# Graph layers and experts on one core: segment columns computed in the instruction's own address, nine of the last ten tiles scattered in three bf16 parts, the residual added on TensorE, the last moments read from PSUM

## The reference, cut to what matters

```python
def _layernorm(x, axis=-1, eps=1e-05):
    m = jnp.mean(x, axis=axis, keepdims=True)
    v = jnp.var(x, axis=axis, keepdims=True)
    return (x - m) / jnp.sqrt(v + eps)

def _L1_gnn_ref(x_nodes, x_edges, path_coeffs, src, dst, path_indices):   # 64 paths, 16 segments of 32
    x1 = x_nodes[src].reshape(-1, N_SEG, EXTENT)
    x2 = x_edges.reshape(-1, N_SEG, EXTENT)
    i1, i2, i3 = (path_indices[:, 0], path_indices[:, 1], path_indices[:, 2])
    contrib = path_coeffs[None, :, None] * x1[:, i1, :] * x2[:, i2, :]
    edge_out = jnp.zeros((x2.shape[0], N_SEG, EXTENT), x_nodes.dtype).at[:, i3, :].add(contrib)
    out = jnp.zeros((n_nodes, OP_SIZE), x_nodes.dtype).at[dst].add(edge_out.reshape(-1, OP_SIZE))
    return out

x = x + _L0_gnn_ref(_layernorm(x), edge_index, ...)
x = x + _L0_ffn_ref(_layernorm(x)[None], ...)[0]
x = x + _L1_gnn_ref(_layernorm(x), edge_attr_512, L1_gnn_path_coeffs, src, dst, L1_gnn_path_indices)
x = x + _L1_ffn_ref(_layernorm(x)[None], L1_ffn_controller, L1_ffn_f1, L1_ffn_f2)[0]
```

## Time and profile before

| | |
|---|---|
| median of the runs | 307.92 us (307.78 to 309.34) |
| the profiled execution | 308.1 us, its span 306.2 us |
| busy in the span | PE 93%, DVE 74%, ACT 45%, POOL 16% |
| chain that ended last, by engine | PE 82%, DVE 5%, issue 5%, ACT 5% |
| first layers, up to the first path | 0 to 101 us |
| block 0, block 1, block 2 | about 101 to 148.7, 148.7 to 206.6, 206.6 to 250.7 us |
| last block's sums to the first transposes | 250.7 to 268.9 us |
| rest of the fourth layer and the store | to 306.2 us |

### The profile page before, as it was taken

One profiled execution on the slowest core, in us unless ns is written; L12 is line 12 of the kernel. 1 busy time (PEld: TensorE's weight loads), 2 busy tenths in 40 slices (PEclk: granted clock), 3 DMA queues, 4 the chain that ended last, 5 costly groups with the idle time before them and its releaser, 6 DMA issues.

```text
span 306.2 us, 5935 instructions
## 1 busy us (share of the span) xinstructions
PE 284.9 (93%) x1720; PEld 198.3 (65%) x1720; DVE 225.3 (74%) x640; ACT 137.9 (45%) x274; POOL 48.4 (16%) x49
## 2 busy tenths in 40 slices
PE   5898899999999859999999999989999999999995
PEld 4665498886444559778778676765666554578731
DVE  5968648061348759999999999999999978555231
ACT  3200241112125028875448786769988837012220
POOL 3000030000007730000489900000000022000000
PEclk9999999999999977999999999999999999999999
DMA  6799940000014752233252010003444448000001
GB/s 213 247 407 425 442 171 0 0 3 0 18 50 139 204 140 69 71 110 100 68 158 85 5 32 3 1 0 139 148 147 139 138 113 301 0 2 2 2 0 68
DMA packets 12288, 33.39 MB, mean 109 GB/s; under 512 B 3297, under 2 KB 3298, under 8 KB 12002
## 3 DMA queue, kind: packets, MB, share of 16 engines
q1 hardware_dynamic: 10338, 26.73, 24.3%
q0 software_dynamic: 1920, 6.29, 7.2%
HBM read 31.97 MB, written 1.05 MB: 108 GB/s over the span
## 4 chain that ended last, share of the span: by engine, by line
PE 82%; DVE 5%; issue 5%; ACT 5%; DVEq 1%; DMA 1%; ACTq 0%; SPq 0%
PE psum L1165 16%; PE psum L1116 14%; PE psum L1064 9%; PE psum L1168 7%; PE psum L967 5%; PE psum L1088 4%; PE psum L1093 4%; PE psum L999 3%; PE psum L1222 2%; PE psum L1247 2%; PE psum L1241 2%; PE psum L1014 2%; PE psum L1123 2%; PE psum L1156 1%; ACT prod L519 1%
## 5 line engine op out<-in xcount | busy, mean ns | idle before, releaser
L1116 PE MATMUL psum<-big,dst_oh 128*128 128x512 f32 x116 | 53.9, 593 | 0.0
L418 POOL DMA_INDIRECT big<-xn_rows,big x24 | 38.5, 1606 | 93.5 <-DMA xn_rows<-xn 48.8
L519 ACT ACTIVATE prod<-edges,coef_b 128x320 f32 (+1 forms) x65 | 35.6, 588 | 21.4 <-PE psum L1168 18.9
L864 DVE TENSOR_TENSOR prod<-big,prod 128x320 f32<-128x320 f32 (+1 forms) x65 | 34.0, 523 | 0.1
L1165 PE MATMUL psum<-prod,ident 128*128 128x128 f32 x160 | 32.2, 299 | 0.6 <-issue 0.2
L1165 PEld LDWEIGHTS psum<-prod,ident 128*128 128x128 f32 x160 | 24.9, 197 | 9.3 <-issue 7.4
L1116 PEld LDWEIGHTS psum<-big,dst_oh 128*128 128x128 f32 x116 | 20.2, 191 | 15.9 <-issue 15.8
L1064 PE MATMUL psum<-edges,big 128*128 128x256 f32 x128 | 28.3, 380 | 0.0
L874 DVE TENSOR_TENSOR big<-big,prod 128x64 f32 (+2 forms) x80 | 26.1, 326 | 1.6 <-issue 0.4
L1064 PEld LDWEIGHTS psum<-edges,big 128*128 128x128 f32 x128 | 24.1, 190 | 3.5 <-DVE edges L791 0.3
L519 ACT ACTIVATE xparts<-edges,coef_b 128x320 f32 (+1 forms) x41 | 22.5, 587 | 3.4 <-PE psum L1168 1.4
(11 more groups left out here) (195 smaller groups left out, 488.9 us busy)
## 6 DMA issues: line engine op xcount, KB each, us to landing
big<-in_w SPq DMA_DIRECT2D x3, 2048.0 KB, 15.9
edges<-in_f SPq DMA_DIRECT2D x11, 512.0 KB, 3.3
edges<-in_edge SPq DMA_DIRECT2D x1, 3584.0 KB, 23.9
edges<-in_edge SPq DMA_DIRECT2D x1, 2560.0 KB, 23.0
edges<-in_edge SPq DMA_DIRECT2D x5, 512.0 KB, 3.9
edges<-in_f SPq DMA_DIRECT2D x1, 2560.0 KB, 9.9
big<-in_gnn_w SPq DMA_DIRECT2D x1, 1024.0 KB, 6.4
xs<-in_x SPq DMA_DIRECT2D x1, 512.0 KB, 3.8
```

The source lines that it names most:

```text
L418: nc.gpsimd.indirect_dma_start(out=x1g[b % 2][:, i, :], out_offset=None, in_=xn_rows, in_offset=bass.IndirectOffsetOnAxis(ap=idx_i[:, 0, F ...
L519: nc.scalar.activation(slot(n)[:, 0:BLOCKS[b], :], edges[:, FIRST[b]:FIRST[b] + BLOCKS[b], bass.ds(single_column(words, p), U)], ACT.Copy, ...
L864: nc.vector.tensor_tensor(v, xg[:, 0:tiles, bass.ds(cols[0], U)], v, ALU.mult).then_inc(mults, 1)
L1116: last = mm(bank[2 + h], dst_oh[:, n % DR, h * P:(h + 1) * P], tile_sums(b, t), start=n == 0, stop=False)
```

## The change

It has three parts.

Columns at the instruction. `column` no longer multiplies by 32. The segment number goes straight into the access pattern (`segment`), and the builder puts the factor into the address. `product_columns` is gone: `multiply` works out its column itself, right in front of its instruction, and so after DVE's wait for ACT's slot has been set in program order. PE's column ranges are written in the same way.

The last block. `SPLIT` is 9 instead of 5: only the first tile is scattered in fp32. ACT begins with the parts as soon as the sums are done, copies PE's sums after the second tile, and waits for that copy in front of tile 5, the first one whose sums came from PE (`KEPT_AT`). `sum_parts` takes the whole of `x1g[1]`.

The residual. Two fp32 matmuls with the identity put `xs` into banks 2 and 3 ahead of the first scattered tile, during block 1. At the end DVE takes the moments of each half, and normalises it, straight from PSUM; ACT copies the halves back into `xs` (`keep_x3`), one between the two roots and one behind its transposed copy. PE waits for both copies ahead of line 1199's matmuls.

```diff
-    SPLIT = 5
+    SPLIT = 9
+    KEPT_AT = BLOCKS[2] - KEPT[2] - (BLOCKS[2] - SPLIT)
...
-            return psum[:, bass.ds(k * PT + 4 * 512, PT * U)]
+            return psum[:, 4 * 512:].rearrange("p (s e) -> p s e", e=PT * U)[:, bass.ds(k, 1), :].rearrange("p o e -> p (o e)")
...
-            return nc.s_assert_within(v * U, 0, (NS - 1) * U,
+            return nc.s_assert_within(v, 0, NS - 1,
                                       skip_runtime_bounds_check_because="segment numbers are below the segments")
+
+        def segment(ap, seg):
+            return ap.rearrange("p t (s u) -> p t s u", u=U)[:, :, bass.ds(seg, 1), :].rearrange("p t o u -> p t (o u)")
...
-            copy_sums(NB - 1, 0, 8)
             act.wait_ge(sums, NP * NB)
-            act.wait_ge(block_out, banks_before(NB))
+            act.wait_ge(scattered, FIRST[2])
             for i in range(SPLIT + 1):
+                if i == 2:
+                    copy_sums(NB - 1, 0, 8)
+                if i == KEPT_AT:
+                    act.wait_ge(block_out, banks_before(NB))
...
-            for h in range(H):
-                root_of_variance(3, h)
+            def keep_x3(h):
+                act.wait_ge(xn_ready, 3 * H + h + 1)
+                nc.scalar.activation(xs[:, h, :], bank[2 + h], ACT.Copy).then_inc(x3_ready, 1)
+            root_of_variance(3, 0)
+            keep_x3(0)
+            root_of_variance(3, 1)
             copy_xnT(2, xnT2)
+            keep_x3(1)
...
-            def product_columns(n):
-                b, p = divmod(n, NP)
...
-                cols = [first_column(words[b], p)]
...
-                return [moved(dve, c, (NS - 1) * U) for c in cols]
...
-                nc.vector.tensor_tensor(v, xg[:, 0:tiles, bass.ds(cols[0], U)], v, ALU.mult).then_inc(mults, 1)
+                nc.vector.tensor_tensor(v, segment(xg[:, 0:tiles, :], first_column(words[b], p)), v, ALU.mult).then_inc(mults, 1)
...
-            multiply(0, product_columns(0))
-            cols = product_columns(1)
+            multiply(0)
             for n in range(NP * NB):
                 if n + 1 < NP * NB:
-                    multiply(n + 1, cols)
-                if n + 2 < NP * NB:
-                    cols = product_columns(n + 2)
+                    multiply(n + 1)
                 add(n)
...
             for h in range(H):
                 dve.wait_ge(half_done, h + 1)
-                nc.vector.tensor_tensor(xs[:, h, :], xs[:, h, :], bank[2 + h], ALU.add).then_inc(x3_ready, 1)
-                if h:
-                    normalise(h - 1)
-                dve.wait_ge(x3_ready, h + 1)
-                variance(h)
-            normalise(H - 1)
+                variance(h, x3)
+                normalise(h, x3)
...
+                if n == 0:
+                    for h in range(H):
+                        mm(bank[2 + h], ident[:], xs[:, h, :], start=True, stop=False)
...
+            pe.wait_ge(x3_ready, H)
```

More of the change, by code:

```diff
@@ L155, in graph_and_experts @@
         rest_sums = [sum_room[0][:, KEPT[0]:, :], sum_room[1], sum_room[0][:, KEPT[2]:, :]]
-        take = carve(x1g[1][:, KEPT[1]:, :].rearrange("p t f -> p (t f)"))
+        take = carve(x1g[1].rearrange("p t f -> p (t f)"))
         sum_parts = take([SPLIT, 3, D], BF16)
@@ L601, in link, with variance, normalise @@
                 dve.wait_ge(chain, links[0])
-            def variance(h):
-                link(nc.vector.bn_stats(out=stats[:, h, :], in_=xs[:, h, :]))
+            def variance(h, of=xs[:]):
+                link(nc.vector.bn_stats(out=stats[:, h, :], in_=of[:, h, :]))
                 nc.vector.bn_aggr(out=mv[:, h, :], in_=stats[:, h, :]).then_inc(var_ready, 1)
-            def normalise(h):
+            def normalise(h, of=xs[:]):
                 lns[0] += 1
@@ L611, in normalise @@
                 link(nc.vector.reciprocal(rstd[:, h:h + 1], root[:, h:h + 1]))
-                nc.vector.tensor_scalar(xn[:, h, :], xs[:, h, :], mv[:, h, 0:1], rstd[:, h:h + 1],
+                nc.vector.tensor_scalar(xn[:, h, :], of[:, h, :], mv[:, h, 0:1], rstd[:, h:h + 1],
                                         ALU.subtract, ALU.mult).then_inc(xn_ready, 1)
@@ L830, in _, with multiply @@
             words += [[None] * len(words[0]) for _ in range(1, NB)]
-            def product_columns(n):
+            def multiply(n):
                 b, p = divmod(n, NP)
@@ L836, in product_columns @@
                     words[b][p] = moved(dve, words[b - 1][p], NS ** 6 - 1)
-                cols = [first_column(words[b], p)]
[L838 to L841, removed]
-                return [moved(dve, c, (NS - 1) * U) for c in cols]
-            def multiply(n, cols):
-                b, p = divmod(n, NP)
+                if b and p % 6 == 0 and direct(b, p):
+                    words[b][ROW_PATHS + p // 6] = moved(dve, words[b - 1][ROW_PATHS + p // 6], NS ** 6 - 1)
                 tiles, xg = BLOCKS[b], x1g[b % 2]
@@ L858, in multiply @@
                         dve.wait_ge(psums, n + 1 - SLOTS)
+                    i2 = single_column(words[b][ROW_PATHS:], p)
                     nc.vector.scalar_tensor_tensor(
-                        out=v, in0=xg[:, 0:tiles, bass.ds(cols[0], U)], scalar=coef_b[:, p:p + 1],
-                        in1=edges[:, FIRST[b]:FIRST[b] + tiles, bass.ds(cols[1], U)], op0=ALU.mult, op1=ALU.mult).then_inc(mults, 1)
+                        out=v, in0=segment(xg[:, 0:tiles, :], first_column(words[b], p)), scalar=coef_b[:, p:p + 1],
+                        in1=segment(edges[:, FIRST[b]:FIRST[b] + tiles, :], i2), op0=ALU.mult, op1=ALU.mult).then_inc(mults, 1)
                     return
                 dve.wait_ge(scaled, sum(not direct(*divmod(m, NP)) for m in range(n + 1)))
-                nc.vector.tensor_tensor(v, xg[:, 0:tiles, bass.ds(cols[0], U)], v, ALU.mult).then_inc(mults, 1)
+                nc.vector.tensor_tensor(v, segment(xg[:, 0:tiles, :], first_column(words[b], p)), v, ALU.mult).then_inc(mults, 1)
             def add(n):
@@ L1113, in scatter @@
                     pe.wait_ge(block_out, banks_before(b + 1))
+                if n == 0:
+                    for h in range(H):
+                        mm(bank[2 + h], ident[:], xs[:, h, :], start=True, stop=False)
                 pe.wait_ge(dst_made, n + 1)
                 for h in range(H):
-                    last = mm(bank[2 + h], dst_oh[:, n % DR, h * P:(h + 1) * P], tile_sums(b, t), start=n == 0, stop=False)
+                    last = mm(bank[2 + h], dst_oh[:, n % DR, h * P:(h + 1) * P], tile_sums(b, t), start=False, stop=False)
                 last.then_inc(scattered, 1)
```

8 lines of the change are left out of this document (5 added, 3 removed).

## The result

| | before | after |
|---|---|---|
| median of the runs | 307.92 us (307.78 to 309.34) | 305.81 us (304.78 to 305.98) |
| ratio to before, 95% interval | | 0.9908 (0.9879 to 0.9938) |
| profiled execution, its span | 308.1, 306.2 us | 305.83, 304.0 us |
| start of the last sum | 250.36 us | 245.51 us |
| start of half 1's transposes | 270.81 us | 268.56 us |

2.1 us faster, of 2.7 forecast. The profile gives the two halves of that: the last sum starts 4.85 us sooner (3.2 forecast), and the way from it to half 1's transposes takes 23.05 us instead of 20.45, 2.6 more (0.5 forecast). Starts are compared with starts here. Behind the transposes the two kernels run alike.

A forecast was written before the change was run, and what follows sets the result against it. Block 0's pace was taken as bound by DVE's register work, blocks 1 and 2 by data; -3.2 + 1.0 - 0.5 = -2.7 us on 308.1 gave 305.4, median 305.2 us, range 303.4 to 308.8.

The forecast's parts named there:

- Part 1, columns: DVE's path loop, block 0: one register instruction and one step fewer in each of 46 paths, 3.2 us saved.
- 0.045 us a step: Register step price from the direct paths, where four steps less take the pace from 0.82 to 0.64 us.
- forecast paces of 0.55, 0.60 and 0.54: Block 0's us per path after the change, for its stretches paced at 0.62, 0.67 and 0.61 before.
- The upper bound of 4.7: Most the columns could save in block 0, in us, as the pace can't pass the data's 0.54 us a path.
- rival three: Block 0 reaches the data's floor, an instruction costing more than 0.026 us: 4.7 us saved, 303.7 us; chance 0.12.
- Rival one: Register work doesn't set block 0's pace, so the columns save nothing: 308.4 us, or 306.8 with half the gain; chance 0.20.
- Part 2, the residual: Two fp32 matmuls on PE at block 1's first scattered tile, 1.72 us, priced at nothing; 1.7 us if slack is gone.
- Part 3, nine split tiles: Tail behind the last sum: four fp32 tiles saved, eaten by PE's two waits of 2.7 us; price +1.0 us.
- the case given with 0.5 us more: In the tail, POOL's mask stretches DVE's work by one more operation, so PE ends 0.5 us later.
- Rival two: PE's clock drops to half in the tail: +3.4 us, 308.6 us, or 312 if it falls twice; chance 0.12.
- clearly after 257: Deciding point for the clock drop: the third part of split tile two coming clearly after 257 us.
- Part 4, moments: Moments and normalisation from PSUM behind the split tiles: gain about 0.5 us, bounds 0 and 1.2.

The follow-up runs named there:

- the wait filled: The changed kernel with 22 matmuls on zeros in PE's wait behind its fp32 tile: 299.36 us, ratio 0.9857; in a later set 299.04 us, 0.9852.
- the second set: The changed kernel, 304.97 us, and it with the third register instruction back, 308.1, one register step more, 304.64, or seven split tiles, 300.93.
- the first and third sets: Columns alone 298.69 us; changed kernel 300.76, with wait filled 299.36 and 299.04, mask later 298.82, five split tiles 297.77, register move 301.15, seven split tiles, mask later 296.78.
- columns alone: The kernel before with only the columns part and its segment addressing, tail as before: 298.69 us, ratio 0.9831.

## Why the prediction came out, point by point

**Part 1, columns: right mechanism, too small.** Taken 3.2 us. The 46 paths gained 4.24, and 0.46 came behind block 0, where the prediction had nothing. The last sum starts 4.85 us sooner; the other 0.15 is 0.58 us ahead of the first sum less 0.43 in the first 16 paths. It can't be put down to the change, since both stretches vary as much between executions of one kernel: with the wait filled the first sum starts at 102.67 us once and at 101.50 the other time, and the first 16 paths of the changed kernel take 15.70 and 14.63 us.

The term that was mis-sized is the price of 0.07 us a path, from "0.045 us a step" and "0.026" for an instruction, which divided the direct paths' saving by all steps alike. "Their price is in no row" was wrong: the rows above show 0.17 us less register work a path. Of the forecast paces of 0.55, 0.60 and 0.54 the first and the last came true, and the middle one is 0.57. That the total of the register work counts, and that a path takes the longer of two sums, the rows bear out to within 0.03 us. The upper bound of 4.7, taken from the data's floor, was the better guess (rival three): the loop now stands at that floor from path 45 on, and 0.03 above it before. Rival one, no gain, is out: 0.53 went to 0.41 us. Each direct path became 0.1 us shorter outside the stall. The prediction counted nothing for them, and with the stall among them no gain can be told.

**Part 2, the residual: right.** Nothing shows; PE has 55.26 busy of 57.00 us in block 1 and DVE's pace is unchanged.

**Part 3, nine split tiles: right at full clock, by another route.** Taken +1.0, measured +1.33 at full clock. The prediction had two waits, 2.7 us together; there is one, of 2.84, since DVE's third subtraction took 2.00 us beside the mask, so that tile one was ready later. That was the case given with 0.5 us more. The second tile was then ready in time (ready near 252.3, PE at it from 252.4 at full clock).

**Rival two: it came in part.** The clock fell where the prediction put it, for 3.4 us instead of 6.7, and cost 1.5 to 1.65 us instead of 3.4. So one of the prediction's own signs of being wrong is there, a second stretch at 0.5 past the last sum. The Trainium skill (TensorE: Matmul & The Clock Gate, "HAM oscillation — how this bites in real kernels") warns of this; the traces agree in direction, not each time: one execution of six kept its clock. The point "clearly after 257" was wrong; the single wait sufficed.

**Part 4, moments: right in direction.** Taken 0.5, measured 0.31 and 0.32. The normalisation takes 0.81 us from PSUM and 0.55 from SBUF, so half 1's transposes wait 0.21 us for DVE behind PE's 12 matmuls. The Trainium skill (VectorE: DVE Perf Modes, "Why PSUM operands drop a tier") said that this operand costs the faster rate: the trace agrees, with 0.26 us a half, 0.52 for both, where the prediction's estimate from it had 0.5 in all. The sum of the prediction left this out, and half 1's transposes come 4.08 us behind the last tile, where the layout had 3.8.

**The sum.** The last sum comes 4.85 us sooner. The tail grew by 2.60 us; the experiments account for it with +1.33 for the split tiles, -0.31 for the moments and 1.5 to 1.65 for the clock, 2.52 to 2.67. Together that is -2.25, as the spans of the two profiled executions differ (306.2 and 304.0). Forecast was -2.7. That the median came within 0.6 us of the forecast is luck: the columns gave 1.5 to 1.65 us more than forecast and the clock took 1.5 to 1.65 that the forecast didn't have, and these two errors cancelled.

## What to carry to other kernels

Read what stands between two instructions of an engine against the time that their data need. If it is more and nothing is waited for, look up the rows of the register instructions by their source lines and add them to the time between them: if that is the pace, register work is the bound, and each instruction less shortens it until the data's need is reached. A price must be measured where that work is the bound; beside data that take longer, most of it hides. When work is taken off an engine by preparing it elsewhere (split tiles), give the engine enough old work to cover the first preparation. Of the three numbers tried, the best was the one where the last old tile ends as the first new one is ready (7: tail 19.24 us), and nine cost more than it saved (21.41 at full clock, against 20.07 for five). A wait of PE ahead of a burst of matmuls, 2.84 us here, is priced twice: as the wait, and as the clock that may fall behind it.

## What was not expected of the hardware

- The register instructions of DVE's sequencer take 0.036 us (a plain move), 0.046 (the product's before) to 0.22 us (a column's division, remainder, multiplication and copy), and 0.05 to 0.09 us lie between two of them. A multiplication more inside one is 0.02 us. Of a move's 0.09 us a path only 0.01 shows beside data that need 0.54.
- POOL's mask stretches DVE's subtractions of 512 columns in SBUF from 0.68 us to 2.00, and a copy of 128 columns from 0.22 to 1.35.
- The stall near 107 us went with the chip: the profiles of the kernel before and of the changed kernel and the four of the second set have it, and none of the eight of the first and third sets. There PE and DVE ran on at full clock, as this window of columns alone shows, with as much traffic as in the row above that has it:

```profile
107.50:112.10 4.60, 4.54 (x28) 3.55 (x28) 4.50 (x15) 3.70 (x8) 2.11 (x2) 1.00 0.66 199
```

The kernel before takes 303.5 to 303.7 us on those chips and 307.1 to 307.9 on the others. What is waited for is not in the profile ("issue"), so the cause is open.
